# Linear-attention layers: the second feed-forward and two quarters of the output projection placed as one run across a step's end, and the second norm's transposes moved to the projection's PSUM bank

## What is computed

```python
for i in range(8):
    residual = x
    Q  = elu(x @ Wq[i] + bq[i]) + 1
    Kf = elu(x @ Wk[i] + bk[i]) + 1
    V  = x @ Wv[i] + bv[i]
    KV, sumK = sum(Kf * V, tokens), sum(Kf, tokens)
    att = Q * KV / (Q * sumK + 1e-6)              # 16 heads x 64 = 1024 columns
    x = layer_norm(gelu(att @ Wo[i] + bo[i]) + residual) * ln1_s[i] + ln1_b[i]
    residual = x
    h = gelu(x @ W1[i] + b1[i])                   # 512 columns
    x = layer_norm(gelu(h @ W2[i] + b2[i]) + residual) * ln2_s[i] + ln2_b[i]
```

## Time and profile before

| | us |
|---|---|
| median of 3 runs | 3348.28 (3346.37 to 3350.55) |
| the profiled execution | 3335.85 |
| its span, first to last instruction | 3334.1 |
| TensorE busy in the span | 3009.8 (90%) |
| VectorE busy | 2779.0 (83%) |
| ScalarE busy | 2464.2 (74%) |
| mean granted TensorE clock | 0.952 |

### The profile page before, as it was taken

The page is one execution under the profiler, slowest core; times in us unless marked ns, Lnnn a source line. Parts: engine busy times, 40 slices in busy tenths (PEclk is TensorE's granted clock), DMA queues, the critical chain, the costliest instruction groups (busy, mean ns, idle before and its releaser), DMA issues. The chain is left out here.

```text
span 3334.1 us, 49450 instructions
## 1 busy us (share of the span) xinstructions
PE 3009.8 (90%) x14448; PEld 1983.6 (59%) x14448; DVE 2779.0 (83%) x11011; ACT 2464.2 (74%) x4579; POOL 590.2 (18%) x715
## 2 busy tenths in 40 slices
PE   7999998282899999999999999999999999999669
PEld 5777776271566666566666656656666666666344
DVE  6878786854689999999999999998989999998456
ACT  6878786132588888888888888888788788888435
POOL 0000001275011111111111111111211211211124
PEclk9999998595899999999999999999999999999859
DMA  1000000323000000000000000000000000000000
GB/s 55 1 1 1 1 0 7 108 37 90 1 1 1 7 26 1 3 31 1 1 7 26 1 4 29 1 1 7 26 1 7 26 1 2 15 1 1 0 1 26
DMA packets 35120, 46.39 MB, mean 14 GB/s; under 512 B 5768, under 2 KB 26304, under 8 KB 34880
## 3 DMA queue, kind: packets, MB, share of 16 engines
q1 hardware_dynamic: 29248, 39.47, 3.6%
q0 software_dynamic: 5632, 4.20, 1.0%
HBM read 35.16 MB, written 8.49 MB: 13 GB/s over the span
## 5 line engine op out<-in xcount | busy, mean ns | idle before, releaser
L1880 DVE TENSOR_SCALAR t_feat_q<-t_recip,t_neg_mean 128x256 f32<-128x256 f32 x1024 | 385.9, 439 | 130.8 <-ACT t_recip L1723 130.7
L1554 PE MATMUL t_o_ps<-t_feat_q,t_wo 128*128 128x512 f32 x1024 | 474.1, 596 | 2.7 <-DVE t_feat_q L1880 2.7
L1715 ACT ACTIVATE t_recip<-t_feat_q,t_z_scale 128x256 f32<-128x256 f32 x1024 | 434.7, 498 | 3.5 <-DVE t_feat_q L1880 2.7
L1701 ACT ACTIVATE t_exp_k<-t_k_ps 128x1024 f32<-128x1024 f32 x256 | 259.4, 1013 | 232.1 <-PE t_k_ps L1528 232.1
L1843 DVE CUSTOM_DVE_ANT_0 t_junk<-t_v_ps,t_feat_k 128x256 f32<-128x256 f32 x1024 | 390.6, 419 | 8.0 <-PE t_v_ps L1528 7.9
L1833 DVE SCALAR_TENSOR_TENSOR t_feat_k<-t_exp_k,t_k_ps 128x256 f32<-128x256 f32 x1024 | 369.0, 416 | 22.1 <-ACT t_exp_k L1701 22.1
L1705 ACT ACTIVATE t_exp_q<-t_q_ps 128x1024 f32<-128x1024 f32 x256 | 261.6, 1022 | 95.4 <-PE t_q_ps L1528 93.0
L1869 DVE SCALAR_TENSOR_TENSOR t_feat_q<-t_exp_q,t_q_ps 128x1024 f32<-128x1024 f32 x256 | 312.7, 1221 | 8.8
L2008 POOL TENSOR_TENSOR t_var_eps<-t_moments,t_ln_eps 128x4 f32<-128x4 f32 x128 | 69.1, 540 | 1301.0 <-DVE t_moments L1891 1301.0
L1554 PEld LDWEIGHTS t_o_ps<-t_feat_q,t_wo 128*128 128x128 f32 x1024 | 194.6, 190 | 176.1 <-issue 155.0
L1526 PE MATMUL t_v_ps<-t_x_hi,t_w_hi 128*128 128x512 f32 x512 | 265.0, 518 | 10.1 <-DVE t_sum_kv L1843 9.1
(11 more groups left out here) (363 smaller groups left out, 7335.7 us busy)
## 6 DMA issues: line engine op xcount, KB each, us to landing
t_raw_w<-in_wq SPq DMA_DIRECT2D x8, 512.0 KB, 3.6
t_raw_w<-in_wk SPq DMA_DIRECT2D x8, 512.0 KB, 5.5
t_raw_w<-in_wv SPq DMA_DIRECT2D x8, 512.0 KB, 6.3
t_wo<-in_wo SPq DMA_DIRECT2D x32, 128.0 KB, 2.2
x<-in_x SPq DMA_DIRECT2D x4, 512.0 KB, 8.7
tokens_dram<-r_hn SPq DMA_DIRECT2D x8, 256.0 KB, 2.3
e_w_raw<-in_fc_w SPq DMA_DIRECT2D x4, 512.0 KB, 4.0
e_w<-in_fc_w SPq DMA_DIRECT2D x4, 512.0 KB, 4.9
```

What stands on the lines that cost most here:

```text
L1554: last = pe.matmul(o_ps[:], wo[:, chunk, :], feat_q[:, s, chunk, :], start=(chunk == 0), stop=(chunk == NC - 1), skip_group_check=True)
L1701: act.activation(exp_k[:], k_ps[:], ACT.Exp, bias=-1.0).then_inc(c["k_exp"], 1)
L1715: last = act.activation(recip[:, q % 2, k * UNIT + n * SEQ:k * UNIT + (n + 1) * SEQ], feat_q[:, s, chunk, cols], ACT.Ln, bias=1.0, scale=z ...
L1880: last = dve.tensor_scalar(feat_q[:, s, chunk, cols], recip[:, q % 2, k * UNIT + n * SEQ:k * UNIT + (n + 1) * SEQ], -1.0, neg_mean[:, s, n ...
```

## The change

Four things change in TensorE's list, and the readers on ScalarE and VectorE follow the bank.

1. W2 moves from between V(1,1) and V(2,0) to the end of the step, behind V(2,1). It no longer waits for `state_t`.
2. P0 moves from behind F(3) to the beginning of the next step, ahead of P1, so W2, P0 and P1 stand in a row. P0 gets the wait for `state_t`.
3. Tz2 and Tn2 write `o_ps` in place of `m0`; `state_t`, the second norm's statistics and its normalisation read `o_ps`.
4. Tz2 moves ahead of F(2), and waits for the read of `o_ps` by the first gelu (`y1_ready`).

```diff
             def project(u, s, q):
                 if q == 0:
                     pe.wait_ge(c["y1_ready"], u + 1)
+                    if u >= 3:
+                        pe.wait_ge(c["state_t_ready"], u - 3 + 2 + PER)
...
-            def second_feed_forward(u, follows):
+            def second_feed_forward(u):
...
-                if follows:
-                    pe.wait_ge(c["state_t_ready"], u - 1 + 2 + PER)
...
                 if C:
+                    project(t - 2, s, 0)
                     project(t - 2, s, 1)
...
+                if E:
+                    pe.wait_ge(c["z2_ready"], t - 4 + 2)
+                    pe.wait_ge(c["y1_ready"], min(t - 2, UNITS - 1) + 2)
+                    turn(o_ps, y2, c["z2_turned"])
                 if Dn:
                     first_feed_forward(t - 3, 2)
...
-                if B:
-                    project(t - 1, r, 0)
-                if E:
-                    pe.wait_ge(c["z2_ready"], t - 4 + 2)
-                    if Dn:
-                        pe.wait_ge(c["hid_ready"], 4 * (t - 3) + 5)
-                    turn(m0, y2, c["z2_turned"])
...
-                    turn(m0, y2, c["n2_turned"])
+                    turn(o_ps, y2, c["n2_turned"])
                 if A:
                     values(t, s, 1, 1)
-                if Dn:
-                    second_feed_forward(t - 3, E)
...
                     values(t, s, 2, 1)
+                if Dn:
+                    second_feed_forward(t - 3)
...
-                    act.activation(g["state_t"][...], m0[:].unsqueeze(1), ACT.Identity,
+                    act.activation(g["state_t"][...], o_ps[:].unsqueeze(1), ACT.Identity,
...
-                    layernorm_stats(t - 4, 1, m0, ...)
+                    layernorm_stats(t - 4, 1, o_ps, ...)
...
-                    normalise(t - 4, 1, m0, y2, ...)
+                    normalise(t - 4, 1, o_ps, y2, ...)
```

More of the change, by code:

```diff
@@ L1784, in step @@
                     act.wait_ge(c["n2_turned"], t - 4 + 2)
-                    act.activation(g["state_t"][:, bass.ds(place_of(t - 4), 1), :], m0[:].unsqueeze(1), ACT.Identity,
+                    act.activation(g["state_t"][:, bass.ds(place_of(t - 4), 1), :], o_ps[:].unsqueeze(1), ACT.Identity,
                                    bias=param(t - 4, 9), scale=param(t - 4, 8)).then_inc(c["state_t_ready"], 1)
@@ L1959, in step @@
                 if E:
-                    layernorm_stats(t - 4, 1, m0, c["z2_turned"], c["bn2_done"], c["stats2_ready"])
+                    layernorm_stats(t - 4, 1, o_ps, c["z2_turned"], c["bn2_done"], c["stats2_ready"])
                 if C:
@@ L1967, in step @@
                 if E:
-                    normalise(t - 4, 1, m0, y2, c["rstd2_ready"], c["n2_ready"])
+                    normalise(t - 4, 1, o_ps, y2, c["rstd2_ready"], c["n2_ready"])
                 if C:
```

## The result

| | before | after |
|---|---|---|
| median, us | 3347.32 (3346.04 to 3350.55) | 3653.39 (3648.94 to 3660.30) |
| ratio | 1 | 1.0939, 95% interval 1.0913 to 1.0966 |
| the profiled execution, its span, us | 3335.85, 3334.1 | 3648.94, 3647.2 |
| mean granted clock over the whole span | 0.952 | 0.915 |

The changed kernel is 9.4% slower: 3653 us where the forecast said 3654, of 3550 to 3705.

The account below looks back on a forecast made before the run. Bound: a loop through TensorE, ScalarE and VectorE, not TensorE alone. Profiled 3335.85 us + 239 (longer steps) + 66 (clock) = 3641 us, or 3654 us on the median's footing; range 3550 to 3705 us.

Parts of the forecast that it names:

- The loop: Linear-attention step as a cycle Q(0), ScalarE, VectorE, B(3), K(3), Q(3), Q(0): +3.98 us a step, +239 us over 60 steps.
- the run to Tn1: TensorE between Q(3) and Q(0): W2, P0 and P1 in a row put 5.13 us more on the path.
- the drain: The last four steps of the layers: taken as 0, ±5 us.
- W2 out of the gap: Between V(1,1) and V(2,0): new TensorE stall of about 2.6 us, B(3) only 0.73 us earlier.
- The early turn: Second norm's turn ahead of F(2): V(0,1) reaches VectorE 0.29 us late, a 0.22 us wait goes, net 0.07 us later.
- P0 out of the first half: TensorE ahead of Q(2): losing P0's 1.71 us there gains 0, because ScalarE is never idle.
- The clock: TensorE's granted clock in the layers: a fall in most steps, 1.1 us of 0 to 1.62 each, +66 us.
- a clock that stays up: Rival, TensorE clock in the layers: same loop without falls, 3588 us; chance 0.28.
- the exchange steps: Steps with a weight exchange: B(0) waits covered against V(2,1) held back, taken as 0, ±13 us.
- a first half that is TensorE's: Rival, step ahead of Q(2): P0's 1.71 us count, so 2.27 us a step, 3485 us; chance 0.05.
- the faster case: Rival, V(2,0) and B(3): banks empty by 2016.9, only two waits go, −55 us, 3293 us; chance 0.05.
- Two falls a step: Rival, TensorE clock: low clock lasts through W2, P0, P1, costing 3.24 us a step, 3783 us; chance 0.05.

Follow-up runs that it names:

- e4: Changed kernel with three extra matmuls, read by nobody, filling the stall between V(1,1) and V(2,0): 3553.99 us, ratio 1.0643 to before.
- e1: Changed kernel with W2 put back between V(1,1) and V(2,0): 3360.59 us, ratio 1.0078 to before.
- e3: Kernel before with P0 alone moved to the beginning of the next step: 3439.60 us, ratio 1.0286 to before.
- e5: Changed kernel with the stall filled by three unread matmuls and the second norm's turn Tz2 back behind F(3): 3555.72 us, ratio 1.0626 to before.
- e6: Changed kernel, not filled, with VectorE's first-norm statistics moved behind the features of K(2): 3518.33 us, ratio 1.0517 to before.
- e8: Kernel before with W2 alone moved to the step's end and three unread matmuls between V(1,1) and V(2,0): 3469.05 us, ratio 1.0377 to before.
- e2: Kernel before with W2 alone moved to the step's end: 3593.52 us, ratio 1.0766 to before.
- e7: Kernel before with VectorE's first-norm statistics moved behind the features of K(2): 3332.97 us, ratio 0.9953 to before.

## Why the prediction was right, point by point

Each leg of the loop can be read off, before from the earlier trace rows (a step being 35.09 us), after from the rows above; B(3) to the run is taken from e4, where the clock is at full speed:

| leg | before, us | changed, us | difference | forecast |
|---|---|---|---|---|
| exp of Q(0) to exp of Q(2), ScalarE | 19.27 | 19.29 | +0.02 | 0 |
| exp of Q(2) to B(3), VectorE and V(2,0) | 7.20 | 6.34 | −0.86 | −0.66 |
| B(3) to the run, at full clock | 3.94 | 3.93 | −0.01 | 0 |
| the run to Tn1 | 1.71 | 6.87 | +5.16 | +5.13 |
| Tn1 to B(0) | 0.94 | 0.53 | −0.41 | −0.49 |
| B(0) to exp of Q(0) | 2.03 | 2.03 | 0 | 0 |
| sum | 35.09 | 38.99 | +3.90 | +3.98 |

Such legs, taken from start to start round a step that repeats, add up to the step by themselves (35.09; with the 5.47 us of the low clock in place of 3.93 the 40.53 of the step shown); the test is that each leg changed as forecast. The second mark, the exponential of Q(2), is only a place to measure from: the work passes from ScalarE to VectorE at attention quarter 0, 10.8 us behind the exponential of Q(0) in both kernels. **The loop** is thus borne out leg by leg, and shown by e1, e3, e5, e6 and e8: each removes or adds one known piece, and each step length came within 0.1 us of what that piece says. In the 59 steps ahead of the drain the 3.91 us make 231 us, where 60 steps of 3.98 were put down as 239.

**W2 out of the gap**: the stall of 2.6 us before V(2,0) is 2.54 from start to start (2009.62 to 2012.39 less one interval), released by the reduction as forecast; the one before B(3) is 0.40 with the features of K(2) as its cause. B(3) came 0.2 us earlier than the forecast: 0.09 of it since a matmul started 0.06 us after VectorE's last read and not 0.15; the other 0.1 comes from VectorE's list, at the wait for the second norm's turn. The features of Q(1) and the statistics behind them, the second row of the kernel before standing in the earlier trace rows (2011.19) and the other two in the changed kernel:

```profile
2009.75 1.22 DVE L1869 SCALAR_TENSOR_TENSOR t_feat_q<-t_exp_q,t_q_ps 128x1024 f32<-128x1024 f32 x1
```

```profile
2003.05 1.22 DVE L1867 SCALAR_TENSOR_TENSOR t_feat_q<-t_exp_q,t_q_ps 128x1024 f32<-128x1024 f32 x1
2004.19 0.88 DVE L1885 BATCH_NORM_STATS2 t_stats<-t_o_ps 128x6 f32<-128x128 f32 x4
```

From start to start that is 1.44 us before and 1.14 after, so the wait was worth 0.30 us, and not the 0.22 of its bracket that the prediction took. **The early turn** costs 0.29 us of V(0,1), as forecast (e5). What it was to win in exchange, that wait, does not hang on the early place: in e5, with the turn behind F(3), the distance is 1.14 us as well. **P0 out of the first half** is worth nothing by itself (e3); its place is now B(2)'s wait of 0.98 us.

**The clock** is the term that was mis-sized. A fall in most steps was right, its price was not: 66 us were put down at 1.1 us a step, on the argument that part of the low stretch lies on the stall. In the step shown it doesn't: the low stretch begins after the stall and costs 1.54 us between B(3) and W2 (5.47 against 3.93). In 19 of the 51 low stretches it does, as in the step at 1971.28, but those are the longer kind, and such plain steps take 41.1 to 41.3 us, 2.1 to 2.3 above e4's 39.00: a fall that began on the stall was dearer, not cheaper. The six plain steps of 38.06 us have no fall; each follows an exchange step with two low stretches. In the 59 steps the clock costs 92 us (after less e4, first to last `state_t`, without the drain), 1.56 a step, near the 1.62 that the earlier trace rows had given for a whole fall and that I had cut down. On the mean the two bounds held, and the value between them should have been near the upper one; in single steps the upper one did not hold. The rival of a clock that stays up gave 3588 us; e4, which is that case, stands at 1.0643, or 3563 us on the footing of the forecast.

**What made up for it**: the exchange steps came out 8 us better in e4 (about 3.4 us a layer over the plain step, where it was 4.6), inside the ±13, and the drain 10.6 us better (86.5 us for the last four intervals, 97.2 before), outside the ±5. The part ahead of and behind the layers added 9 us. So 231 + 92 − 8 − 11 + 9 = 313 us, as measured between the spans, against 305 forecast: the loop was 8 us too dear, the clock 26 too cheap, and the terms put at nothing gave 10 back. Between profiled executions the forecast was thus 8 us low (3641 against 3648.94); that the medians agree to 1 us is luck, since the profiled execution of before lies 0.34% below its median and that of after 0.12%.

**The rivals**: a first half that is TensorE's, and the faster case, in which VectorE empties both banks by 2016.9, are excluded by the rows above. Two falls a step at 3.24 us did not come about: the longer low stretches cost up to 2.3 us in a plain step of after, and e2 pays 1.8 on the mean.

## What to carry to other kernels

A TensorE that is 97% busy need not be the bound: close the step into its loop through the other engines first, and ask of every instruction that is moved whether it stood in time that the loop leaves free anyway. W2 stood there and cost 0.73 of its 3.42 us; at the step's end it cost its whole length. A stall that is made in this way is to be charged with its clock as well, at the full price of a fall, and an engine's order inside the loop (here 1.2 us of statistics) can be worth as much as its work.

## What the runs showed of the hardware that was not expected

**Short stalls bring the clock down.** In after nearly every step has its fall at idle times of 2.38 and 0.40 us around one values block, during the first in some steps and behind the second in others. In e6 the idle times of a plain step are 1.18 and 0.42 us and there are 24 falls, so they follow in some steps and not in others; in e3 a single one of 2.01 us brings a fall in the exchange steps, and one of 1.68 us in only one of 38 plain steps. So the length of the longest idle time alone doesn't tell whether the clock falls. The Trainium skill ("TensorE: Matmul & The Clock Gate", section "Why this matters for your kernels") asks that gaps between bursts stay short, and by its rule all of these are short enough to be harmless; after, e2, e3 and e6 disagree, and e4 shows that filling the gap with products that nobody reads is worth 99 us.

**The part behind the layers differs from kernel to kernel with the same instructions.** The stretch from the last `state_t` to the end, before, and in e2 and e8 (columns as in rows 1):

```profile
3180.90:3334.00 153.10, 126.11 (x472) 73.72 (x472) 102.62 (x237) 66.97 (x124) 55.28 (x53) 0.76 0.05 14
```

```profile
3419.20:3587.00 167.80, 140.86 (x472) 79.82 (x472) 103.16 (x237) 67.06 (x124) 55.17 (x53) 0.68 0.05 13
```

```profile
3315.80:3463.80 148.00, 121.04 (x472) 71.85 (x472) 102.48 (x237) 66.98 (x124) 55.29 (x53) 0.79 0.05 15
```

The same 472 matmuls take 148.0 to 167.8 us at clocks of 0.79 to 0.68. That is up to 20 us, 0.6% of the kernel, in a part whose instructions are the same; what sets the clock there is open, and for an edit in the layers step lengths are the safer measure.

**VectorE's tensor-scalar slows beside GpSimd.** All 1024 attention instructions of the kernel before (minimum, median and maximum in ns, first and last start), and GpSimd's splits at the time of the quarter that took 3.29 us:

```profile
L1880 DVE TENSOR_SCALAR t_feat_q<-t_recip,t_neg_mean x1024: 320/347/1457, 871.1 to 3132.1; 128x256 f32<-128x256 f32 x171
```

```profile
2055.33 1.28 POOL L2015 TENSOR_TENSOR t_x_lo<-state_t,t_x_hi 128x512 fp32r<-128x512 f32 x1 [1.69 <-ACT t_x_hi L1686]
...
2057.58 1.29 POOL L2004 TENSOR_TENSOR t_w_lo<-t_raw,t_w_hi 128x512 fp32r<-128x512 f32 x1
```

The quarter from 2055.73 to 2059.02 lies on GpSimd's subtractions for the state (2055.33) and, in the exchange step, for W1's remainder (2057.58); in e7 it starts at 2046.21, ahead of them, and takes 1.11 us. Of the 1024, the 867 that lie beside no tensor operation of GpSimd take 346 ns on the mean and 357 at most; the 157 that lie beside one take 952 on the mean. Of those, 132 take over 600 ns, and 125 of these end 0.14 to 0.16 us after GpSimd's instruction does, so VectorE waits for that instruction to end. The Trainium skill ("SBUF — State Buffer", section "Who interferes with whom") says that VectorE and GpSimd share a pair of ports under an exclusive lock; the trace agrees, by these ends. That this sharing, and not something else in that step, is what e7 gained from is argued from these rows; no run removed GpSimd's work alone.
